# Splits ahead of what waits for the output projection, x loaded one group ahead, one store per head pair

## The chip, the cores and the metric

The kernel runs on one core of a Trainium2 chip. The metric is the time of one execution on the device in microseconds, the median of several runs. One more execution was recorded by the profiler; every row below is of that one. TensorE (PE; PEld is its weight load), VectorE (DVE), ScalarE (ACT) and GpSimd (POOL) compute, and SyncE (SP) issues all DMA transfers on one queue.

## The reference

Three blocks work on x, 64 sequences of 32 tokens with 512 features: cross attention to 257 context rows of 384 features per sequence, self attention with a relative position bias, and a quantised feed-forward network. The change touches the first one alone.

```python
def cross_attention(hidden_states, encoder_hidden_states, Wq, Wk, Wv, Wo, bo):   # 16 heads of 64
    q = hidden_states @ Wq
    k = encoder_hidden_states @ Wk
    v = encoder_hidden_states @ Wv
    scores = jnp.einsum('bhsd,bhkd->bhsk', q, k) * scale
    probs = jax.nn.softmax(scores, axis=-1)
    out = jnp.einsum('bhsk,bhkd->bhsd', probs, v)
    return out.transpose(0, 2, 1, 3).reshape(B, S, H * Dh) @ Wo + bo
...
x = x + cross_attention(_layernorm(x), ctx_768, ...)
x = x + self_attention(_layernorm(x), ...)
x = x + ffn(_layernorm(x), ...)
```

## The kernel before

Each engine has its own program, written out by hand, and semaphores order them. The eight PSUM banks (s0, s1, t0, t1, o0, o1, q0, q1) are handed round by a table: `full` waits until TensorE has filled a bank, `taken` until its reader has drained it. TensorE works in two-part arithmetic: every operand is kept as a high part, which ACT copies out, and a low part, the rest, which DVE subtracts out after it.

**Projection stage** (`*_project_all`). The 16 tiles of 128 tokens are taken in 4 groups. For each group x is loaded into one buffer `x_in` (`load_x_group`), normalised on DVE (`dve_group_stats` in the middle of the Q projections, `dve_group_norm` later; its step is counted in `s_xp`), transposed, multiplied by Wq (`Q`, eight units), and then by Wk of each head (`QK`, eight head pairs, units of 3 chunks x 2 heads), so that later the scores are taken directly against the context rows. The order of a group on TensorE is Q 0 to 3, QK 0 to 3, Q 4 to 7, transposes of the next group's x, QK 4 to 7. ACT copies the even head of a pair into the tile `staged`, DVE the odd one; `staged` has 4 slots, one per head pair, and `wait_slot` keeps a slot from being written before its last store has landed. SP stores each pair to `qk_by_tile` in DRAM, once it is complete, with one DMA per head (L1209), in rows of 1.5 KB.

**Main stage** (`*_cross_tile`). A tile is four batches, b = 0 to 3. For a batch TensorE makes scores against the context in four row groups (units S, bank order s0, s1, q0, s0), transposes of the probabilities of the batch before (PT, PL), their product with the context (PV 0 to 2), and three transposed chunks of the next context (CT 0 to 2). DVE takes row maxima (L1063), ACT the exponentials (L796), and a bank of scores is free when its exponential is done. In batch 1 the value projection W of the tile before is made, in batch 3 its output projection WO (L642), which stands between PV 1 and CT 2. DVE adds the residual to WO in `dve_x_out` (L1056). CT chunks are copied by ACT (L692) and DVE (L856) into `cT`; the chunk c = 2 is needed by the last three of the nine matmuls of the first scores of the next batch.

The projected q of tile t+1 lies in `raw` (one load of 3 MB, in batch 0 of tile t, after the last split has been done) and is split in batch 3 of tile t into `qk`: four high parts on ACT (`act_qk_high`, L730) and four low parts on DVE (`dve_qk_low`, L987), one per row group. GpSimd splits the context rows of each batch (`pool_split`, L1152 and L1155), after the last PV of the batch before; SP loads the context two batches ahead into one of two buffers `c_raw` after that (`load_ctx`, L1174).

In the lines of the tensors below, `c_raw_89` is the buffer of the even batches and `c_raw_98` of the odd ones.

Of the kernel before, what the change touches and what calls it, by code (L numbers as in the profile page):

```python
# [14 lines left out]
P = 128  # L15
# [133 lines left out]
def build_kernel(nc, x, ctx_768, Wq, Wk, Wv, Wo, bo, a_Wq, a_Wk, a_Wv, a_Wo, rel_emb, clip_x, clip_down,  # L149
# [22 lines left out]
    with ctx:  # L172
# [52 lines left out]
        assert sb.at <= STAGED  # L225
        staged = early("staged", [P, 4, 2, GROUP, HB], F32)
        x_in = early("x_in", [P, GROUP, D], F32)
# [469 lines left out]
        def wait_slot(eng, s, j):  # L697

            if 2 * s + j // 4:
                eng.wait_ge(s_staged[j % 4], 32 * (2 * s + j // 4))  # L700

# [7 lines left out]
        def act_group_qk(act, s, j):  # L709
            wait_slot(act, s, j)  # L710
            for c in range(KC):
                ps, free = full(act, project(("QK", s, j, c, 0)))
                nc.scalar.activation(staged[:, j % 4, 0, :, c * P:(c + 1) * P], tokens_of(ps), ACT.Copy).then_inc(free, 1)

# [12 lines left out]
        def act_qk_high(act, t, rg):  # L727

            act.wait_ge(s_qraw, 16 * t + 16)
            nc.scalar.activation(qk[:, 0, rg, :, :, :].rearrange("p c b (h q) -> p h (c b) q", h=4),  # L730
                                 raw[:, rg, :, :].rearrange("p h (a q) -> p h a q", q=SQ), ACT.Copy).then_inc(s_qhi, 1)

# [57 lines left out]
        def act_cross_tile(act, t, section):  # L790
# [16 lines left out]
            for b in range(4):  # L807
# [26 lines left out]
                act_last_scalars(act, b, 4 * t)  # L834
                if after:
                    ctxT(b, 2)
                if b == 3 and more:
                    act_qk_high(act, t + 1, 2)
                    act_qk_high(act, t + 1, 3)
                if section == "first" and b in (1, 2):  # L840
                    act_wo_high(act, b - 1)
# [120 lines left out]
        def dve_group_qk(dve, s, j):  # L962
            wait_slot(dve, s, j)
            for c in range(KC):
                ps, free = full(dve, project(("QK", s, j, c, 1)))
                nc.vector.tensor_copy(staged[:, j % 4, 1, :, c * P:(c + 1) * P], tokens_of(ps)).then_inc(free, 1)

# [13 lines left out]
        def dve_qk_low(dve, t, rg, section=None):  # L981

            if section:
                full(dve, U1(("S", 3, rg), t - 1, section))
            dve.wait_ge(s_qhi, 4 * t + (rg + 1))
            part = [qk[:, i, rg, :, :, :].rearrange("p c b (h q) -> p h (c b) q", h=4) for i in range(2)]
            nc.vector.tensor_tensor(part[1], raw[:, rg, :, :].rearrange("p h (a q) -> p h a q", q=SQ), part[0].bitcast(F32),  # L987
                                    ALU.subtract).then_inc(s_qlo, 1)
# [69 lines left out]
        def dve_cross_tile(dve, t, section):  # L1058
# [19 lines left out]
            for b in range(4):  # L1078
# [33 lines left out]
                if before:  # L1112
                    dve_attended(dve, t, b, 1, section)
                if b == 3 and begun:
                    dve_x_out(dve, t, section)
                if after:
                    ctxT(b, 2)
                if qk_next:
                    dve_qk_low(dve, t + 1, 2, section)
                if before:  # L1120
                    dve_attended(dve, t, b, 2, section)
                if qk_next:
                    dve_qk_low(dve, t + 1, 3, section)
                if section == "first" and b >= 2:
# [54 lines left out]
        def load_qk(sp, t, ahead):  # L1179
            later = qk_dram[ahead:]  # L1180
            one = later[t:t + 1] if isinstance(t, int) else later[bass.ds(t, 1)]
            sp.dma_start(raw[:].rearrange("p r h n -> p (r h n)"), one.rearrange("a p r h n -> p (a r h n)")).then_inc(s_qraw, 16)

        def sp_project_all(sp):
# [8 lines left out]
            load_ctx(sp, 0, 0)  # L1193
            load_ctx(sp, 0, 1)
            for s in range(GROUPS):
                if s < GROUPS - 1:
                    sp.wait_ge(s_xp, GROUP * (s + 1))
                    load_x_group(sp, s + 1)
                if s == 2:
                    sp.wait_ge(s_wqlo, 2)  # L1200
                    for i in range(4):
                        sp.wait_ge(s_staged[i], 64)
                    load_qk(sp, 0, 0)
                for j in range(8):
                    for c in range(KC):
                        for par in range(2):
                            taken(sp, project(("QK", s, j, c, par)))
                    for par in range(2):
                        sp.dma_start(qk_dram[GROUP * s:GROUP * (s + 1), :, 2 * (j // 4) + par, j % 4, :].rearrange("t p n -> p t n"),  # L1209
                                     staged[:, j % 4, par, :, :]).then_inc(s_staged[j % 4], 16)  # L1210
            for i in range(4):
                sp.wait_ge(s_staged[i], 64 * GROUPS)
            sp.dma_start(wv[:], Wv.rearrange("(k p) n -> p k n", p=P)).then_inc(s_wvo, 16)
# [4 lines left out]
        def sp_cross_tile(sp, t, section):  # L1218
            begun, more = section != "first", section != "last"
            for b in range(4):  # L1220
                if more or b < 2:
                    sp.wait_ge(s_nat, 4 * t + (b + 1))
                    load_ctx(sp, 4 * t, b + 2)
# [745 lines left out]
```

## Time and profile before

| | |
|---|---|
| median of 3 runs | 1853.93 us (1853.47 to 1854.21) |
| the profiled execution | 1855.51 us, span 1853.7 us |
| busy share: PE, DVE, ACT, POOL | 91%, 65%, 42%, 17% |
| mean granted TensorE clock | 0.956 |
| moved by DMA | 185.31 MB, 100 GB/s over the span |

The span is the time from the first to the last instruction on the core. A busy share counts instructions in flight over the whole span. The granted clock is given as a share of 2.4 GHz. The projection stage ends near 219 us, the main stage near 1172 us; tiles 1 to 14 are one loop, of which each pass is some 59 us.

### The profile page before, as it was taken

To read this page: it belongs to the slowest core of one execution; us is meant where nothing else is said; L and a number is where in the kernel's file an instruction comes from. 1 tells how busy PE (TensorE), PEld (TensorE's weight loads), DVE (VectorE), ACT (ScalarE), POOL (GpSimd) and SP (SyncE) were. 2 spreads that over 40 slices of the span, in tenths; PEclk is the share of its full clock that TensorE was granted. 3 is DMA by queue.
4 is the path that set the end of the run, shared out by engine and by line. 5 is a ranking of instruction groups with operands and counts; after the bars stand their busy time and mean duration, and the time that the engine had idled before them with its cause. 6 is when DMAs were issued, how large, how long until landed. Compare 5 with 4: busy or idle time off the path is not lost.

```text
span 1853.7 us, 38185 instructions
## 1 busy us (share of the span) xinstructions
PE 1693.4 (91%) x13767; PEld 1443.9 (78%) x13767; DVE 1207.7 (65%) x2675; ACT 780.8 (42%) x1699; POOL 315.7 (17%) x179
## 2 busy tenths in 40 slices
PE   6798879999999999999999999899999999996888
PEld 5677768888888888888888888789899998983333
DVE  6556656676666756666566666467777786646686
ACT  3343644445544544454544544232222222223556
POOL 0000022223222223232222223100000000000334
PEclk9998988999999999999999999999999999997899
DMA  4788852321222212221222212411111111003002
GB/s 168 271 288 309 310 194 95 105 105 37 102 105 105 95 37 103 105 105 39 100 105 105 75 55 75 176 53 40 45 40 45 40 45 35 17 23 113 31 16 91
DMA packets 81663, 185.31 MB, mean 100 GB/s; under 512 B 5008, under 2 KB 54224, under 8 KB 79568
## 3 DMA queue, kind: packets, MB, share of 16 engines
q1 hardware_dynamic: 81616, 184.68, 28.3%
q8 instruction: 30, 0.49, 0.1%
q14 instruction: 17, 0.14, 0.0%
HBM read 121.74 MB, written 62.91 MB: 100 GB/s over the span
## 4 chain that ended last, share of the span: by engine, by line
PE 53%; issue 31%; DVE 8%; ACT 3%; DMA 3%; SPq 1%; POOL 1%; DVEq 0%; ACTq 0%; POOLq 0%
PE psum_o L614 15%; PE psum_s L583 10%; PE psum_o L629 5%; PE psum_q L642 5%; PE psum_o L495 4%; PE psum_q L583 3%; PE psum_t L554 2%; DVE qk L987 2%; PE psum_t L594 2%; PE psum_o L1545 2%; DMA x_in<-in_x_dram 2%; PE psum_s L1545 2%; ACT qk L730 1%; PE psum_q L511 1%; PE psum_q L601 1%
## 5 line engine op out<-in xcount | busy, mean ns | idle before, releaser
L614 PE MATMUL psum_o<-pT,c_nat 128*128 128x512 f32 x1152 | 333.9, 430 | 10.3 <-issue 9.1
L583 PE MATMUL psum_s<-cT,qk 128*128 128x258 f32 x1728 | 256.7, 294 | 42.4 <-ACT probs L796 38.4
L583 PEld LDWEIGHTS psum_s<-cT,qk 128*128 128x128 f32 x1728 | 229.5, 194 | 55.7 <-ACT probs L796 39.0
L614 PEld LDWEIGHTS psum_o<-pT,c_nat 128*128 128x128 f32 x1152 | 219.7, 204 | 53.0 <-issue 12.1
L1152 POOL TENSOR_TENSOR c_nat<-c_raw,zero 128x768 fp32r<-128x768 f32 x64 | 94.9, 1483 | 899.2 <-PE psum_o L614 672.3
L1047 DVE SCALAR_TENSOR_TENSOR oT<-p_last,c_last,psum_o 128x512 f32<-128x512 f32 x192 | 142.8, 744 | 88.9 <-PE psum_o L614 88.7
L796 ACT ACTIVATE probs<-psum_s,nmax 128x257 f32<-128x257 f32 x192 | 91.8, 478 | 250.4 <-DVE nmax L1063 250.3
L987 DVE TENSOR_TENSOR qk<-raw,qk 128x1536 fp32r<-128x1536 f32 x64 | 141.0, 2205 | 15.9 <-ACT qk L730 15.6
L1155 POOL TENSOR_TENSOR c_nat<-c_raw,c_nat 128x768 fp32r<-128x768 f32 x64 | 140.8, 2200 | 5.0
L692 ACT ACTIVATE cT<-psum_t 128x256 fp32r<-128x256 f32 x192 | 68.3, 389 | 171.9 <-PE psum_t L554 171.5
L856 DVE TENSOR_TENSOR pT<-psum_t,pT 128x512 fp32r<-128x512 f32 x128 | 87.7, 686 | 71.0 <-ACT pT L692 71.0
L1267 PEld LDWEIGHTS psum_o<-xnT,w2q 128*128 128x128 f32 x1024 | 116.7, 192 | 2.4 <-issue 1.2
L1267 PE MATMUL psum_o<-xnT,w2q 128*128 128x128 f32 x1024 | 117.0, 275 | 1.0 <-issue 1.0
L1267 PE MATMUL psum_q<-xnT,w2k 128*128 128x128 f32 x1024 | 117.0, 275 | 0.0
L1267 PEld LDWEIGHTS psum_q<-xnT,w2k 128*128 128x128 f32 x1024 | 115.6, 192 | 0.0
L1063 DVE TENSOR_REDUCE nmax<-psum_s 128x1 f32<-128x257 f32 x192 | 80.4, 419 | 40.0 <-PE psum_s L583 40.0
L495 PE MATMUL psum_o<-xnT,wq 128*128 128x512 f32 x384 | 93.0, 402 | 4.9 <-DVE xnT L856 2.6
L730 ACT ACTIVATE qk<-raw 128x1536 fp32r<-128x1536 f32 x64 | 93.7, 1493 | 0.0
L495 PEld LDWEIGHTS psum_o<-xnT,wq 128*128 128x128 f32 x384 | 73.6, 194 | 23.4 <-issue 4.4
L629 PE MATMUL psum_o<-oT,wv 128*64 128x128 f32 x1536 | 90.7, 275 | 1.0 <-DVE oT L1047 1.0
L629 PEld LDWEIGHTS psum_o<-oT,wv 128*64 128x64 f32 x1536 | 83.2, 137 | 6.1 <-issue 4.0
L583 PE MATMUL psum_q<-cT,qk 128*128 128x258 f32 x576 | 82.7, 288 | 4.9 <-DVE qk L987 4.9
(225 smaller groups left out, 3098.3 us busy)
## 6 DMA issues: line engine op xcount, KB each, us to landing
qk_by_tile<-staged SPq DMA_DIRECT2D x64, 768.0 KB, 8.4
raw<-qk_by_tile SPq DMA_DIRECT2D x16, 3072.0 KB, 10.3
c_raw<-in_ctx_dram SPq DMA_DIRECT2D x64, 384.0 KB, 3.1
out_dram<-x_out SPq DMA_DIRECT2D x32, 256.0 KB, 2.0
x_in<-in_x_dram SPq DMA_DIRECT2D x4, 1024.0 KB, 10.4
x_res<-in_x_dram SPq DMA_DIRECT2D x16, 256.0 KB, 2.6
x_ln<-out_dram SPq DMA_DIRECT2D x16, 256.0 KB, 2.7
x_res<-out_dram SPq DMA_DIRECT2D x16, 256.0 KB, 2.9
```

The source lines that it names most:

```text
L495: m = pe.matmul(ps[:], wq[:, part, k, j * P:(j + 1) * P], xnT[:, moving, k, :, :], start=(k, part, moving) == (0, 0, 0), stop=(k, part) == ...
L583: m = pe.matmul(ps[:, 0:SKP], qk[:, part, rg, c, b, :], cT[b % 2][:, moving, c, :], start=(c, part, moving) == (0, 0, 0), stop=(c, part) = ...
L614: i = pe.matmul(ps[:], c_nat[(b - 1) % 2][:, part, k, m * P:(m + 1) * P], pT[:, moving, k, :], start=(k, part, moving) == (0, 0, 0), stop= ...
L629: i = pe.matmul(ps[64 * par:64 * par + 64, h4 * P:(h4 + 1) * P], wv[:, c, head * DH:(head + 1) * DH], oT[:, c, slot, :, :], start=c == 0, ...
L642: i = pe.matmul(ps[:], a[part][:, k, :], w[moving][:, k, :], start=(k, part, moving) == (0, 0, 0), stop=(k, part) == (KI - 1, 1))
L730: nc.scalar.activation(qk[:, 0, rg, :, :, :].rearrange("p c b (h q) -> p h (c b) q", h=4), raw[:, rg, :, :].rearrange("p h (a q) -> p h a ...
L796: nc.scalar.activation(probs[b % 2][:, rg, 0:SK], bank[bk][:, 0:SK], ACT.Exp, bias=nmax[:, rg:rg + 1], accum_out=den[:, rg:rg + 1]).then_i ...
L987: nc.vector.tensor_tensor(part[1], raw[:, rg, :, :].rearrange("p h (a q) -> p h a q", q=SQ), part[0].bitcast(F32), ALU.subtract).then_inc( ...
L1047: nc.vector.scalar_tensor_tensor(oT[:, m, :, (b - 1) % 4, :], p_last[:].rearrange("p (s q) -> p s q", q=SQ), c_last[:, (b - 1) % 2, m:m + ...
L1152: G.tensor_tensor(flat(c_nat[i][:, 0, :, :]), flat(c_raw[i][:]), zero[:].to_broadcast([P, 2 * DC]), ALU.add).then_inc(s_chi, 1)
L1155: G.tensor_tensor(c_nat[i][:, 1, :, :], c_raw[i][:], c_nat[i][:, 0, :, :].bitcast(F32), ALU.subtract).then_inc(s_nat, 1)
L1267: i = pe.matmul(ps[:, j * P:(j + 1) * P], w[:, k, (4 * n + j) * P:(4 * n + j + 1) * P], xnT2[:, k, :], start=k == 0, stop=k == KD - 1)
```

## The change

It has four parts.

The splits: in batch 3 of a tile, ACT makes the high parts of row groups 2 and 3 before it copies the third context chunk, and DVE makes their low parts directly behind the second attended chunk, ahead of `dve_x_out`, the third context chunk and the last attended chunk.

The loads of x: from group 2 on, x is loaded after the first four head pairs of the group two before have been stored, as soon as the group between has been normalised, and no longer at the start of the next group.

The stores: `staged`, `qk_by_tile` and `raw` have the two heads of a pair side by side, and one DMA stores both, in rows of 3 KB. The semaphore thresholds are halved.

The context of batch 2 of the first tile is loaded directly behind the last stores of the projection stage, ahead of the output and value weights.

```diff
-        staged = early("staged", [P, 4, 2, GROUP, HB], F32)
+        staged = early("staged", [P, 4, GROUP, 2, HB], F32)
...
             if 2 * s + j // 4:
-                eng.wait_ge(s_staged[j % 4], 32 * (2 * s + j // 4))
+                eng.wait_ge(s_staged[j % 4], 16 * (2 * s + j // 4))
...
                 act_last_scalars(act, b, 4 * t)
-                if after:
-                    ctxT(b, 2)
                 if b == 3 and more:
                     act_qk_high(act, t + 1, 2)
                     act_qk_high(act, t + 1, 3)
+                if after:
+                    ctxT(b, 2)
...
                     dve_attended(dve, t, b, 1, section)
+                if qk_next:
+                    dve_qk_low(dve, t + 1, 2, section)
+                    dve_qk_low(dve, t + 1, 3, section)
                 if b == 3 and begun:
                     dve_x_out(dve, t, section)
                 if after:
                     ctxT(b, 2)
-                if qk_next:
-                    dve_qk_low(dve, t + 1, 2, section)
                 if before:
                     dve_attended(dve, t, b, 2, section)
-                if qk_next:
-                    dve_qk_low(dve, t + 1, 3, section)
...
             load_ctx(sp, 0, 1)
+            sp.wait_ge(s_xp, GROUP)
+            load_x_group(sp, 1)
             for s in range(GROUPS):
-                if s < GROUPS - 1:
-                    sp.wait_ge(s_xp, GROUP * (s + 1))
-                    load_x_group(sp, s + 1)
...
-                    for par in range(2):
-                        sp.dma_start(qk_dram[GROUP * s:GROUP * (s + 1), :, 2 * (j // 4) + par, j % 4, :].rearrange("t p n -> p t n"),
-                                     staged[:, j % 4, par, :, :]).then_inc(s_staged[j % 4], 16)
+                    pair = qk_dram[GROUP * s:GROUP * (s + 1), :, j % 4, 2 * (j // 4):2 * (j // 4) + 2, :]
+                    sp.dma_start(pair.rearrange("t p r n -> p t (r n)"),
+                                 staged[:, j % 4, :, :, :].rearrange("p t r n -> p t (r n)")).then_inc(s_staged[j % 4], 16)
+                    if j == 3 and s < GROUPS - 2:
+                        sp.wait_ge(s_xp, GROUP * (s + 2))
+                        load_x_group(sp, s + 2)
+            sp.wait_ge(s_nat, 1)
+            load_ctx(sp, 0, 2)
             for i in range(4):
-                sp.wait_ge(s_staged[i], 64 * GROUPS)
+                sp.wait_ge(s_staged[i], 32 * GROUPS)
...
-                if more or b < 2:
+                if (more or b < 2) and (begun or b):
                     sp.wait_ge(s_nat, 4 * t + (b + 1))
                     load_ctx(sp, 4 * t, b + 2)
```

On DVE, at the end of the loop over the tiles (batch 3), the change moves these rows:

```order
-L1056 TENSOR_TENSOR x_out<-psum_q,x_res 128x512
-L855 REGISTER_ALU
-L856 TENSOR_TENSOR cT_87<-psum_t,cT_87 128x256
 L985 REGISTER_ALU
 L987 TENSOR_TENSOR qk<-raw,qk 128x4x12x32
-L1047 SCALAR_TENSOR_TENSOR oT<-p_last,c_last,psum_o 128x16x32
 L985 REGISTER_ALU
 L987 TENSOR_TENSOR qk<-raw,qk 128x4x12x32
...
+L1056 TENSOR_TENSOR x_out<-psum_q,x_res 128x512
+L855 REGISTER_ALU
+L856 TENSOR_TENSOR cT_87<-psum_t,cT_87 128x256
+L1047 SCALAR_TENSOR_TENSOR oT<-p_last,c_last,psum_o 128x16x32
```

Both low splits of q now stand ahead of the residual addition, the third context chunk and the last attended chunk.

On SP, from the load of x for group 1 to the load of q for tile 1, the rows were these before:

```order
L1177 DMA x_in<-in_x_dram 128x4x512
L1209 DMA qk_by_tile<-staged 128x4x384 x16
L1177 DMA x_in<-in_x_dram 128x4x512
L1209 DMA qk_by_tile<-staged 128x4x384 x16
L1177 DMA x_in<-in_x_dram 128x4x512
L1182 DMA raw<-qk_by_tile 128x6144
L1209 DMA qk_by_tile<-staged 128x4x384 x32
L1213 DMA wv<-in_L_xattn_Wv_dram 128x3x1024
L1214 DMA wo_raw<-in_L_xattn_Wo_dram 128x8x512
L1215 DMA bo_all<-in_L_xattn_bo_dram 128x512
L1216 DMA x_res<-in_x_dram 128x512
L1174 DMA c_raw_89<-in_ctx_dram 128x2x384
```

And in the changed kernel, whose lines have other numbers there, up to the same weights:

```order
L1176 DMA x_in<-in_x_dram 128x4x512
L1207 DMA qk_by_tile<-staged 128x4x768 x4
L1176 DMA x_in<-in_x_dram 128x4x512
L1207 DMA qk_by_tile<-staged 128x4x768 x8
L1176 DMA x_in<-in_x_dram 128x4x512
L1207 DMA qk_by_tile<-staged 128x4x768 x4
L1181 DMA raw<-qk_by_tile 128x6144
L1207 DMA qk_by_tile<-staged 128x4x768 x16
L1173 DMA c_raw_89<-in_ctx_dram 128x2x384
L1216 DMA wv<-in_L_xattn_Wv_dram 128x3x1024
L1217 DMA wo_raw<-in_L_xattn_Wo_dram 128x8x512
```

The loads of x stand half a group earlier among the stores, the stores are half as many and twice as wide, and the context load (`c_raw_89`) is ahead of the weights.

## Rows read from the trace of the kernel before

**Rows 1.** Waits in the loop's stretch: us in total, times, longest.
```profile
PE psum_s L583 <- ACT probs L796: 33.5, 14, 2.6
PE psum_q L583 <- DVE qk L987: 4.9, 14, 0.4
```

**Rows 2.** Windows of one tile, cut at its batches 0, 1, 2, 3.
```profile
core 0: us, PE busy (x) PEld busy (x) DVE busy (x) ACT busy (x) POOL busy (x), PEclk, DMA share, GB/s
341.54:357.00 15.46, 12.34 (x72) 10.59 (x71) 12.01 (x20) 7.59 (x20) 4.69 (x2) 0.89 0.71 250
357.00:373.62 16.62, 16.62 (x171) 15.04 (x169) 8.11 (x20) 7.08 (x20) 4.56 (x3) 1.00 0.10 35
373.62:384.09 10.47, 10.47 (x73) 9.57 (x72) 6.74 (x18) 5.66 (x18) 3.31 (x2) 1.00 0.12 38
384.09:399.97 15.88, 15.88 (x97) 14.06 (x96) 10.90 (x21) 8.87 (x21) 3.32 (x2) 1.00 0.09 25
```

**Rows 3.** Windows: 14 tile periods, a stretch behind one wait, self-attention stage.
```profile
341.02:1171.40 830.38, 783.64 (x5707) 696.47 (x5707) 526.82 (x1102) 405.88 (x1086) 222.42 (x126) 0.96 0.25 89
...
349.80:353.20 3.40, 3.02 (x11) 2.44 (x10) 2.48 (x8) 2.70 (x9) 0.00 (x0) 0.50 0.94 340
...
1195.00:1648.00 453.00, 449.45 (x5233) 409.92 (x5232) 321.92 (x920) 115.70 (x181) 0.46 (x1) 1.00 0.12 40
```

**Rows 4.** Timeline between tiles 1 and 2: start, duration, engine, line.
```profile
334.83 0.26 ACT L743 ACTIVATE c_last<-rem_sum 128x3 f32 x1
...
337.24 0.74 DVE L1047 SCALAR_TENSOR_TENSOR oT<-p_last,c_last,psum_o 128x512 f32<-128x512 f32 x1
...
340.13 0.69 DVE L1056 TENSOR_TENSOR x_out<-psum_q,x_res 128x512 f32<-128x512 f32 x1 [2.16 <-PE psum_q L642]
...
340.63 2.85 ACT L730 ACTIVATE qk<-raw 128x1536 fp32r<-128x1536 f32 x2
340.77 0.42 DVE L856 TENSOR_TENSOR cT<-psum_t,cT 128x256 fp32r<-128x256 f32 x1
...
341.54 1.24 PE L583 MATMUL psum_s<-cT,qk 128*128 128x258 f32 x9
...
341.88 1.47 POOL L1152 TENSOR_TENSOR c_nat<-c_raw,zero 128x768 fp32r<-128x768 f32 x1 [12.57 <-PE psum_o L614]
...
345.54 2.72 DVE L987 TENSOR_TENSOR qk<-raw,qk 128x1536 fp32r<-128x1536 f32 x1
...
348.19 0.41 DVE L1063 TENSOR_REDUCE nmax<-psum_s 128x1 f32<-128x257 f32 x1
...
349.25 1.90 PE L583 MATMUL psum_s<-cT,qk 128*128 128x258 f32 x9 [2.38 <-ACT probs L796]
```

**Rows 5.** The low splits of q on DVE: ns min/median/max, first and last start.
```profile
L987 DVE TENSOR_TENSOR qk<-raw,qk x64: 1736/1759/2820, 218.6 to 1116.4; 128x1536 fp32r<-128x1536 f32 x64
```

**Rows 6.** Windows from a group's first QK to its fifth: groups 1, 2, 0.
```profile
80.78:113.82 33.04, 23.90 (x139) 19.80 (x138) 18.30 (x44) 11.21 (x20) 0.00 (x0) 0.85 0.70 244
134.18:167.91 33.73, 24.40 (x138) 20.16 (x138) 18.39 (x44) 11.22 (x20) 0.00 (x0) 0.85 0.91 336
38.60:60.38 21.78, 21.59 (x137) 17.77 (x137) 16.99 (x42) 11.22 (x20) 0.00 (x0) 1.00 0.81 288
```

**Rows 7.** Timeline: the load of x for group 2, and its first reader.
```profile
75.49 2.32 SPq L1177 DMA_DIRECT2D x_in<-in_x_dram  x1
...
88.34 2.47 DVE L916 BATCH_NORM_STATS2 group_stats<-x_in 128x6 f32<-128x512 f32 x4 [8.85 <-DMA x_in<-in_x_dram]
```

**Rows 8.** Windows in which only stores, then only weight loads, are moved.
```profile
95.00:110.00 15.00, 15.00 (x84) 12.60 (x81) 10.25 (x31) 6.55 (x11) 0.00 (x0) 0.93 1.03 363
...
236.00:238.00 2.00, 2.00 (x19) 2.00 (x18) 1.17 (x5) 1.75 (x6) 0.00 (x0) 1.00 1.01 418
```

**Rows 9.** Timeline of TensorE: context transposes of batch 1 and batch 2, first tile.
```profile
248.13 1.11 PE L554 MATMUL psum_t<-ident,c_raw 128*128 128x128 f32 x4 [8.71 <-DMA c_raw<-in_ctx_dram]
...
261.43 0.60 PE L554 MATMUL psum_t<-ident,c_raw 128*128 128x128 f32 x4
```

**Rows 10.** DMA issue of batch 3's context, from about 239.1: KB, us to landing.
```profile
c_raw<-in_ctx_dram SPq DMA_DIRECT2D x1, 384.0 KB, 17.3
```

More of the change, by code:

```diff
@@ L712, in act_group_qk @@
                 ps, free = full(act, project(("QK", s, j, c, 0)))
-                nc.scalar.activation(staged[:, j % 4, 0, :, c * P:(c + 1) * P], tokens_of(ps), ACT.Copy).then_inc(free, 1)
+                nc.scalar.activation(staged[:, j % 4, :, 0, c * P:(c + 1) * P], tokens_of(ps), ACT.Copy).then_inc(free, 1)
         def act_wq_high(act, h):
@@ L730, in act_qk_high @@
             nc.scalar.activation(qk[:, 0, rg, :, :, :].rearrange("p c b (h q) -> p h (c b) q", h=4),
-                                 raw[:, rg, :, :].rearrange("p h (a q) -> p h a q", q=SQ), ACT.Copy).then_inc(s_qhi, 1)
+                                 raw[:, :, rg, :].rearrange("p h (a q) -> p h a q", q=SQ), ACT.Copy).then_inc(s_qhi, 1)
         def act_last_key(act, b, batch):
@@ L965, in dve_group_qk @@
                 ps, free = full(dve, project(("QK", s, j, c, 1)))
-                nc.vector.tensor_copy(staged[:, j % 4, 1, :, c * P:(c + 1) * P], tokens_of(ps)).then_inc(free, 1)
+                nc.vector.tensor_copy(staged[:, j % 4, :, 1, c * P:(c + 1) * P], tokens_of(ps)).then_inc(free, 1)
         def dve_wq_low(dve, h):
@@ L986, in dve_qk_low @@
             part = [qk[:, i, rg, :, :, :].rearrange("p c b (h q) -> p h (c b) q", h=4) for i in range(2)]
-            nc.vector.tensor_tensor(part[1], raw[:, rg, :, :].rearrange("p h (a q) -> p h a q", q=SQ), part[0].bitcast(F32),
+            nc.vector.tensor_tensor(part[1], raw[:, :, rg, :].rearrange("p h (a q) -> p h a q", q=SQ), part[0].bitcast(F32),
                                     ALU.subtract).then_inc(s_qlo, 1)
@@ L1181, in load_qk @@
             one = later[t:t + 1] if isinstance(t, int) else later[bass.ds(t, 1)]
-            sp.dma_start(raw[:].rearrange("p r h n -> p (r h n)"), one.rearrange("a p r h n -> p (a r h n)")).then_inc(s_qraw, 16)
+            sp.dma_start(raw[:].rearrange("p h r n -> p (h r n)"), one.rearrange("a p h r n -> p (a h r n)")).then_inc(s_qraw, 16)
         def sp_project_all(sp):
@@ L1201, in sp_project_all @@
                     for i in range(4):
-                        sp.wait_ge(s_staged[i], 64)
+                        sp.wait_ge(s_staged[i], 32)
                     load_qk(sp, 0, 0)
```

## The prediction

> **What bounds the kernel now.** I looked first at the waits of the main loop (tiles 1 to 15 of the cross attention), because nearly half of the span lies there. TensorE is busy for 783.64 of 830.38 us [rows 3], so it bounds the stage, and what can be saved is what it waits for and what it loses while its clock is halved. Its waits are few and regular: 14 times it waits for ACT's exponential (33.5 us in all, 2.4 us each), 14 times for a low split on DVE (4.9 us, 0.35 each) [rows 1]. Cutting one tile into its four batches shows where: batch 0 takes 15.46 us, batch 2, with the same work, 10.47 [rows 2]. Batches 1, 2 and 3 keep TensorE busy for every microsecond. So 5 us of each tile are lost at its start.
>
> The timeline of that start shows how [rows 4]. At the end of a tile DVE finishes with the second attended chunk at 337.98 (337.24 + 0.74) and then idles 2.16 us for the output projection (WO). ACT has been idle since 335.09. Only after WO do the last two splits of q for the next tile run: high parts on ACT from 340.63, low parts on DVE until 348.26 (345.54 + 2.72). The first row maximum of the new tile stands behind them, at 348.19. Its exponential frees bank s0, so the fourth block of scores, for which TensorE was ready at 346.87, starts at 349.25.
>
> The clock comes on top. Right behind this wait the granted clock is 0.50 (1.2 GHz, from 2.4), and it does not fall once in 453 us of the self-attention stage, where TensorE is busy 449 us [rows 3]. Over the loop the mean is 0.96: about 8% of 830 us, some 66 us, at half speed, which costs 33 us if TensorE has work throughout.
>
> **The moved splits.** I redo the boundary with the durations of the rows [rows 4]. ACT has nothing left to do at 335.09, so the two high splits (2.85 us) end at 337.95, well before the third context transpose reaches ACT. DVE starts the low splits at 337.98. One takes 1.76 us without a neighbour (median of 64), up to 2.82 beside GpSimd [rows 5]; GpSimd's own split starts only at 341.88 and two of DVE's end at 341.4, so 1.76 is the right one, with 0.5 us to spare. Then x_out (0.69) to 342.1, the low part of the third context chunk (0.42) to 342.5, attended chunk 2 (0.74, as the one at 337.24) to 343.2, row maximum to 343.6, exponential to 344.4. TensorE wants bank s0 at 346.5: that wait goes, and so does the one for the third split.
>
> What is late instead is the third context chunk: 342.5 where it was 341.2. TensorE starts the first scores at 341.54 and uses that chunk for the last three of nine matmuls, two thirds of 1.24 us later, at 342.35. I take a new wait of 0.2 us. Its bounds: nothing, and 2.1 us if both splits run beside GpSimd (1.0 each more). Behind the waiting matmul stand only TensorE's own transposes. x_out is stored 1.3 us later, and nobody in the loop waits for that store. The next tile's load of q, gated by the fourth split, only gets earlier.
>
> So batch 0 becomes batch 2 plus 0.2: a tile of 10.67 + 16.62 + 10.47 + 15.88 = 53.64 us. The loop's 830.38 us hold 14 tile periods with one boundary each, 59.31 on average. 14 x (59.31 - 53.64) = **79 us** saved. Of these about 46 are waits (2.4 + 0.35 + a cascaded half microsecond, less 0.2, per tile) and 33 the clock, which I take to stay up because nothing over 0.4 us remains.
>
> The Trainium skill, page "SBUF — State Buffer", section "SBUF: two separate sides", calls the port that DVE and GpSimd share an exclusive lock: the later of the two instructions blocks fully. The rows show the split stretched by 1.0 us at most, less than the 1.5 us of GpSimd's copy. By the page a split caught behind it would be late by the whole copy; by the rows, by 1.0 us.
>
> **x one group ahead.** In the projection stage, group 1 takes 33.04 us from its first QK to its fifth, and group 2 takes 33.73, where group 0 takes 21.78 for the same steps [rows 6]. The reason is one load: x for the next group is issued at 75.49, behind sixteen stores of the group before, and DVE, which takes its statistics in the middle of the Q projections, waits 8.85 us for it until 88.34 [rows 7]. All later copies out of PSUM stand behind, and TensorE with them. In the changed kernel the load goes out when that group's x is normalised, in front of the second four stores: for group 2 a transposition and some two Q projections before group 0's second QKs begin at 60.38, so about 55 us instead of 75. In front of it are at most the last of four stores, and it lands by about 64, some 15 us before DVE asks (88.34 - 8.85 = 79.5). SP now waits for the normalisation ahead of the second four stores, but these need QK results that begin later, at 60.38. Statistics of 2.5 us that now run on time push the copies by 0.3 us. Saved: 33.04 + 33.73 - 2 x 21.78 - 0.3 = **23 us**.
>
> **Rows of 3 KB.** The 32 stores move the same 50 MB. A half group is 6.3 MB, 17.3 us at the 363 GB/s of the stores; loads of longer rows reach 418 [rows 8]. So 3 KB rows save nothing to 2.3 us per half; I take 1.6 (400 GB/s). Nobody waits for a store in this trace, and a half group lasts 21 us, so the gain counts only at the end of the stage. The load of q for tile 0 (3 MB, 7.5 us) now runs into the stores of group 2, since TensorE no longer pauses there: the queue is then some 3 us behind. A slot is written again about 19 us after its store is issued (a half group less the way from the first copy to the store), and the last of four stores lands 3 + 15.7 - 6 + 2 = 15 us after its issue. That hides it; with that cover gone (1.5 KB rows and a queue 7 us behind), one wait of 1 to 3 us.
>
> The Trainium skill, page "DMA: Bandwidth & Descriptors", section "Specifications", puts the HBM limit of a core at 358 GB/s and line rate at 512 B rows; by it the longer rows would give 0. This trace's 418 GB/s is above it, but that is for loads, and no store here has longer rows. The sum would be lower by 1.6 us.
>
> **The context load.** In the first tile TensorE waits 8.71 us for the context of batch 2, until 248.13 [rows 9], because the load stood behind the weights. It now goes ahead of them, directly behind the last stores, and lands near 233, where 239.4 is needed. Late next is the context of batch 3: issued about 239.1, landing 17.3 us later at 256.4 [rows 10]. Everything in front of it starts 1.6 us earlier (stores) and is shorter by one context load (1.0 us), so it lands at 253.8. Its transposes stood at 261.43 [rows 9] and now run then: 7.6 us. On the way ACT waits for the output weights (bo lands last, about 244.7) with some 0.5 us for TensorE, inside this. At the end of this tile a low split of the weights (3.9 us) still keeps DVE, so its boundary gives only about 1 us, and the clock takes about as much back. **7.5 us**.
>
> **Sum.** 79 + 23 + 7.5 = 109.5 us from a span of 1853.7: 1744.2, in the profiled execution's time of 1855.5, 1746. The median of the runs is 1853.93, 1.6 us below that execution: **1744 us**.
>
> **Rivals.**
> *The clock still falls.* The waits go, but each tile still gets one stretch of 3.4 us or more at half speed, from the small waits at the boundary or the idle before it. For it: the loop has one such stretch in every tile. Against: they lie behind the 2.4 us wait. It gives back 1.7 to 2.4 us per tile, 24 to 33: 1768 to 1777. Chance 0.13.
> *GpSimd meets the splits.* If DVE is half a microsecond later than I reckon, its second split runs beside GpSimd, 1.0 us longer, and the first scores wait for the third chunk: 14 x 1.1 = 15 us, 1759. Chance 0.09. By the skill's lock it would be 1.5 us each, 21 us.
> *The change does not do it in the projections.* x still arrives late behind four stores, or a slot wait takes its place: up to 23 us back, 1767. Against: 15 us of slack. Chance 0.05.
> *Slower.* The third context chunk, attended 2 and the first row maximum all stand behind both splits now. Each microsecond by which the splits end after 341.4 is a microsecond of TensorE in the first scores, in each of 14 tiles. The loop's own gain is gone at 5.67 + 0.2 = 5.9 us of delay, all gains at 109.5 / 14 + 0.2 = 8 us; at 9 us the time is 1744 + 14 x 8.8 = 1867. It needs a late q or a held ACT. Against: q is loaded in batch 0 and split in batch 3, with 16.62 + 10.47 us of batches 1 and 2 between [rows 2]. Chance 0.02.
> *Forecast*: 0.71, by itself 1736 to 1754.
>
> **Numbers.** The range has 1732 below (no new wait, clock up in the first tile too, 12 us) and 1778 above (clock still falling). The measurement tells 0.2%, 3.7 us, from no change; every case but the slower one lies beyond it: faster 0.97, same 0.01, slower 0.02.
>
> **What would show it.** In the trace after: periods between stores of x_out near 53.6 us; batch 0 as long as batch 2; TensorE's wait for the exponential gone from the loop, in its place up to 0.2 us for the third chunk; mean clock of the loop 0.99 or 1.00; x in flight from about 55 us, no wait for it; the three group steps alike near 21.8 us; in the first tile a wait of some 3 us for the context of batch 3. I am wrong if the clock keeps falling once per tile, or if GpSimd's split starts before 341.4 on this scale.

## The result and the profile after

| | before | after |
|---|---|---|
| median of the runs | 1853.7 us (4 runs, 1853.13 to 1854.21) | 1738.15 us (4 runs, 1735.61 to 1741.85) |
| ratio, 95% interval | | 0.9378 (0.9359 to 0.9398) |
| profiled execution, its span | 1855.5, 1853.7 us | 1741.85, 1740.0 us |

The changed kernel is 115 us faster; the forecast was 110, and the time lies inside its range. The profiled execution is the slowest of its four runs, so the sums below, made in its time, come to 113.7 us. Line numbers after the change: GpSimd's copies of the context are L1151 and L1154, the stores of the projections L1207, the load of x L1176, that of q L1181, that of the context L1173.

The page of the changed kernel: first the span, then busy time by engine, then two rows of the DMA issues (KB each, median us to landing).

```profile
span 1740.0 us, 38153 instructions
...
PE 1650.0 (95%) x13767; PEld 1414.2 (81%) x13767; DVE 1173.3 (67%) x2675; ACT 779.3 (45%) x1699; POOL 297.3 (17%) x179
...
qk_by_tile<-staged SPq DMA_DIRECT2D x32, 1536.0 KB, 10.4
...
x_in<-in_x_dram SPq DMA_DIRECT2D x4, 1024.0 KB, 7.4
```

**The loop.** The windows of the loop's 14 periods, and of one tile cut at its four batches, in the changed kernel (columns as in [rows 2]).

```profile
310.48:1055.64 745.16, 745.16 (x5701) 671.92 (x5700) 491.19 (x1100) 402.23 (x1084) 202.63 (x126) 1.00 0.27 99
...
363.25:373.89 10.64, 10.64 (x73) 9.62 (x72) 7.35 (x20) 5.65 (x18) 3.31 (x2) 1.00 0.71 269
373.89:390.30 16.41, 16.41 (x170) 14.87 (x169) 8.12 (x20) 7.06 (x20) 4.55 (x3) 1.00 0.25 97
390.30:400.77 10.47, 10.47 (x74) 9.56 (x73) 6.74 (x18) 5.65 (x18) 3.31 (x2) 1.00 0.12 38
400.77:416.60 15.83, 15.83 (x97) 14.05 (x96) 13.37 (x22) 10.81 (x22) 3.32 (x2) 1.00 0.09 25
```

Against [rows 3] the loop is 85.2 us shorter: 46.7 of it is time in which TensorE was idle (830.38 less 783.64, now nothing), 38.5 is busy time (783.64 to 745.16). Most of that is the clock: cut into windows of 0.5 us, the loop before has 68.3 us at 0.50, in one stretch behind each of the 14 boundaries, and the changed loop has none. Half of it, 34.1 us, is the clock's part; the other 4.4 are not separated. Batch 0, 15.46 us in [rows 2], is now 10.64 and nearly as long as batch 2. A tile takes 53.35 us. The trace lists no wait of TensorE in this stretch; both of [rows 1] are gone.

The timeline of the boundary between tiles 1 and 2 in the changed kernel: start, duration, engine, line, and in brackets the idle time ahead and what ended it.

```profile
359.60 3.43 DVE L987 TENSOR_TENSOR qk<-raw,qk 128x1536 fp32r<-128x1536 f32 x2
...
362.93 0.69 DVE L1056 TENSOR_TENSOR x_out<-psum_q,x_res 128x512 f32<-128x512 f32 x1
...
363.25 1.39 PE L583 MATMUL psum_s<-cT,qk 128*128 128x258 f32 x9
...
363.53 0.42 DVE L856 TENSOR_TENSOR cT<-psum_t,cT 128x256 fp32r<-128x256 f32 x1
363.58 1.47 POOL L1151 TENSOR_TENSOR c_nat<-c_raw,zero 128x768 fp32r<-128x768 f32 x1 [12.58 <-PE psum_o L614]
...
367.85 1.32 PE L583 MATMUL psum_s<-cT,qk 128*128 128x258 f32 x9
```

The two splits now fill DVE's idle time ahead of the output projection and end at 363.03, 0.55 us before GpSimd starts (0.5 was reckoned). The first scores take 1.39 us instead of 1.24 [rows 4]: that is the new wait for the third context chunk, 0.15 us. The block at 367.85 is the one that waited 2.38 us in [rows 4]. Over the whole kernel, no split is stretched any more (the largest was 2820 ns in [rows 5]); min/median/max in ns:

```profile
L987 DVE TENSOR_TENSOR qk<-raw,qk x64: 1737/1754/1760, 195.1 to 1001.5; 128x1536 fp32r<-128x1536 f32 x64
```

**The projections.** Windows of groups 1, 2 and 0 in the changed kernel, cut as in [rows 6].

```profile
80.38:102.21 21.83, 21.63 (x137) 18.34 (x136) 16.86 (x42) 11.21 (x20) 0.00 (x0) 1.00 0.82 308
122.61:144.44 21.83, 21.63 (x137) 18.33 (x136) 16.86 (x42) 11.21 (x20) 0.00 (x0) 1.00 1.01 390
38.20:60.01 21.81, 21.61 (x137) 17.60 (x137) 17.01 (x42) 11.22 (x20) 0.00 (x0) 1.00 0.81 301
```

All three are alike. The timeline shows why: the load of x for group 2 is issued at 57.03 us, not at 75.49 [rows 7], and DVE's statistics start with no wait in brackets.

```profile
57.03 0.38 SPq L1176 DMA_DIRECT2D x_in<-in_x_dram  x1
...
79.00 2.46 DVE L916 BATCH_NORM_STATS2 group_stats<-x_in 128x6 f32<-128x512 f32 x4
```

**The first tile.** TensorE's waits there, changed kernel: the 8.71 us for batch 2's context [rows 9] are gone, and 4.33 us for batch 3's took their place. Later DVE's context chunks come late behind its splits of q. The 2.92 us were there before the change too. The 1.37 us are the price of the new order at this tile's end, where TensorE waited 4.2 us for the exponential before.

```profile
232.13 0.66 PE L554 MATMUL psum_t<-ident,c_raw 128*128 128x128 f32 x4 [4.33 <-DMA c_raw<-in_ctx_dram]
...
250.61 0.69 PE L554 MATMUL psum_t<-ident,c_raw 128*128 128x128 f32 x2 [2.92 <-DVE cT L856]
255.80 0.62 PE L583 MATMUL psum_s<-cT,qk 128*128 128x258 f32 x3 [1.37 <-DVE cT L856]
```

**The sum in the trace.** Up to the loop 30.5 us are saved (341.02 less 310.48), in the loop 85.2; behind the loop it is 2.1 us longer (1853.7 − 1171.40 = 682.3, 1740.0 − 1055.64 = 684.4). 30.5 + 85.2 − 2.1 = 113.6.

### The profile page after: what moved, and what is told of

Read it like the earlier page. It is cut to its first block, busy times and chain, and to the rows that moved or that the text cites. A ratio compares the mean times of both kernels' runs of the same rounds, so it can differ in the third digit from the quotient of the medians.

```text
span 1740.0 us, 38153 instructions
## 1 busy us (share of the span) xinstructions
PE 1650.0 (95%) x13767; PEld 1414.2 (81%) x13767; DVE 1173.3 (67%) x2675; ACT 779.3 (45%) x1699; POOL 297.3 (17%) x179
## 4 chain that ended last, share of the span: by engine, by line
PE 60%; issue 30%; DVE 5%; DMA 2%; ACT 2%; POOL 1%; SPq 0%; ACTq 0%; POOLq 0%; DVEq 0%
PE psum_o L614 15%; PE psum_s L583 11%; PE psum_o L629 5%; PE psum_q L642 5%; PE psum_o L495 5%; PE psum_q L583 4%; PE psum_t L594 3%; PE psum_t L554 2%; PE psum_o L1548 2%; PE psum_s L1548 2%; PE psum_q L601 2%; PE psum_t L511 1%; DMA c_raw<-in_ctx_dram 1%; PE psum_q L511 1%; PE psum_s L511 1%
## 5 line engine op out<-in xcount | busy, mean ns | idle before, releaser
L614 PE MATMUL psum_o<-pT,c_nat 128*128 128x512 f32 x1152 | 309.9, 406 | 3.8 <-issue 2.6
L583 PEld LDWEIGHTS psum_s<-cT,qk 128*128 128x128 f32 x1728 | 225.8, 190 | 17.5 <-issue 6.2
L614 PEld LDWEIGHTS psum_o<-pT,c_nat 128*128 128x128 f32 x1152 | 204.2, 190 | 39.2 <-DVE pT L856 3.4
L1151 POOL TENSOR_TENSOR c_nat<-c_raw,zero 128x768 fp32r<-128x768 f32 x64 | 95.4, 1490 | 801.9 <-PE psum_o L614 598.4
L1154 POOL TENSOR_TENSOR c_nat<-c_raw,c_nat 128x768 fp32r<-128x768 f32 x64 | 122.1, 1907 | 5.0
L987 DVE TENSOR_TENSOR qk<-raw,qk 128x1536 fp32r<-128x1536 f32 x64 | 110.6, 1751 | 1.7 <-ACT qk L730 1.5
L1349 PE MATMUL psum_t<-w2o_high,aT 128*128 128x512 f32 x256 | 84.2, 400 | 2.2 <-DVE aT L1451 2.2
```

What stands on the lines that cost most here:

```text
L583: m = pe.matmul(ps[:, 0:SKP], qk[:, part, rg, c, b, :], cT[b % 2][:, moving, c, :], start=(c, part, moving) == (0, 0, 0), stop=(c, part) = ...
L614: i = pe.matmul(ps[:], c_nat[(b - 1) % 2][:, part, k, m * P:(m + 1) * P], pT[:, moving, k, :], start=(k, part, moving) == (0, 0, 0), stop= ...
L987: nc.vector.tensor_tensor(part[1], raw[:, :, rg, :].rearrange("p h (a q) -> p h a q", q=SQ), part[0].bitcast(F32), ALU.subtract).then_inc( ...
L1151: G.tensor_tensor(flat(c_nat[i][:, 0, :, :]), flat(c_raw[i][:]), zero[:].to_broadcast([P, 2 * DC]), ALU.add).then_inc(s_chi, 1)
L1154: G.tensor_tensor(c_nat[i][:, 1, :, :], c_raw[i][:], c_nat[i][:, 0, :, :].bitcast(F32), ALU.subtract).then_inc(s_nat, 1)
```

## The experiments

**1. The moved splits alone, and each half.** `splits_only` is the kernel before with the moves on ACT and DVE:

```diff
 ACT:
-                if after:
-                    ctxT(b, 2)
                 if b == 3 and more:
                     act_qk_high(act, t + 1, 2)
                     act_qk_high(act, t + 1, 3)
+                if after:
+                    ctxT(b, 2)
 DVE:
+                if qk_next:
+                    dve_qk_low(dve, t + 1, 2, section)
+                    dve_qk_low(dve, t + 1, 3, section)
                 if b == 3 and begun:
                     dve_x_out(dve, t, section)
                 if after:
                     ctxT(b, 2)
-                if qk_next:
-                    dve_qk_low(dve, t + 1, 2, section)
                 if before:
                     dve_attended(dve, t, b, 2, section)
-                if qk_next:
-                    dve_qk_low(dve, t + 1, 3, section)
```

Expected: 

> The kernel before with the moved splits alone (ACT's and DVE's), all loads and stores as they were. If the splits do what the sum says, the loop gives all of its gain here: tile periods of 53.4 us instead of 59.3, no wait of TensorE for the exponential in the loop, mean clock of the loop 1.00, about 85 us less than before, 1768 us. If the loop's gain comes in part from the changed transfers (GpSimd's and SP's work meeting the boundary less), periods stay above 54.5 us and the time above 1784. If the waits go but the clock falls all the same, 46 us less: 1808.

Measured: 1763.84 us, ratio 0.9509 (0.9495 to 0.9523), about 91 us saved. Its loop, in the windows:

```profile
338.65:1083.88 745.23, 745.23 (x5701) 672.00 (x5700) 491.17 (x1100) 402.26 (x1084) 202.62 (x126) 1.00 0.27 99
```

745.23 against 745.16 us: the loop's whole gain is the splits'. The rest of the change adds nothing there.

Outside the loop the profiled `splits_only` is 2.4 us shorter ahead of it (341.02 less 338.65) and 2.6 behind it.

`act_half` has only ACT's part of that diff.

Expected: 

> The kernel before with ACT's half of the moved splits alone: the high parts 2 and 3 ahead of ACT's third context chunk, DVE's order as before. DVE's low splits still wait for the output projection, but no longer for ACT: the first starts at 341.2 instead of 342.1 on the scale of rows 4, so the wait of 2.4 us becomes 1.4. 0.95 us in 14 tiles are 13 us, 1840. If the shorter wait no longer makes the clock fall, 33 more: 1807.

Measured: 1799.57 us, ratio 0.9685 (0.9658 to 0.9713), 55 us saved by the medians and 58 by the ratio, more than either case expected (1840 and 1807). The windows, the waits (us in total, times, longest) and the timeline of `act_half` at a boundary:

```profile
338.91:1116.27 777.36, 756.55 (x5707) 677.12 (x5707) 504.58 (x1102) 401.81 (x1084) 234.06 (x126) 0.99 0.26 95
```

```profile
PE psum_o L614 <- issue: 13.0, 14, 0.9
PE psum_s L583 <- ACT probs L796: 7.8, 14, 0.6
```

```profile
394.24 1.75 DVE L987 TENSOR_TENSOR qk<-raw,qk 128x1536 fp32r<-128x1536 f32 x1
...
395.00 2.31 POOL L1152 TENSOR_TENSOR c_nat<-c_raw,zero 128x768 fp32r<-128x768 f32 x1 [12.58 <-PE psum_o L614]
...
396.56 2.37 DVE L987 TENSOR_TENSOR qk<-raw,qk 128x1536 fp32r<-128x1536 f32 x1
```

With the high parts ready early, DVE's third split no longer waits for ACT. It starts before GpSimd's copy instead of behind it, and then it is GpSimd that is stretched (2.31 instead of 1.47 us), while the split keeps its 1.75 (it was 2.8). The earlier start (1.0 us against TensorE's first scores), that microsecond and 0.35 us on the fourth split (2.37 for 2.72, [rows 4]) bring the exponential 2.5 us forward. TensorE itself comes 0.6 us earlier, so 0.55 us of the 2.38 us wait are left. What I had left out of both cases is that who starts first decides who is stretched.

The mean of 0.99 hides something. In windows of 0.5 us the clock still falls behind 3 of the 14 boundaries, 10.2 us in all, and at the other 11 it stays up. One boundary of each kind, with the same two waits ahead (0.55 us for the exponential and 0.94 ahead of the first PV):

```profile
402.50:405.80 3.30, 3.30 (x11) 2.62 (x10) 1.27 (x4) 2.40 (x9) 0.00 (x0) 0.50 1.11 457
458.00:461.30 3.30, 2.35 (x13) 1.93 (x13) 2.16 (x8) 2.94 (x11) 0.00 (x0) 1.00 0.98 343
```

`dve_half` has only DVE's part; it is the slower rival made true, since the low splits now wait for high splits that still follow the output projection.

Expected: 

> The kernel before with DVE's half of the moved splits alone: low parts 2 and 3 ahead of the residual, the third context chunk and the last attended chunk, while ACT still makes the high parts behind its third context chunk, which waits for the output projection. This is the slower rival made true: DVE's splits start at 342.1, run beside GpSimd to 347.6, the third context chunk is ready at 348.7, and TensorE waits in the first scores from 342.35, 6.4 us, with the half clock behind it. Batch 0 becomes 18.6 to 20.3 us instead of 15.5 to 17.6: 40 us more, 1894. If the order on DVE alone made the gain, about 1770.

Measured: 1894.07 us, ratio 1.0205 (1.0185 to 1.0224), as expected. The timeline of `dve_half` at a boundary:

```profile
401.85 6.09 DVE L987 TENSOR_TENSOR qk<-raw,qk 128x1536 fp32r<-128x1536 f32 x2 [4.16 <-ACT qk L730]
...
408.46 0.41 DVE L856 TENSOR_TENSOR cT<-psum_t,cT 128x256 fp32r<-128x256 f32 x1
...
408.93 1.01 PE L583 MATMUL psum_s<-cT,qk 128*128 128x258 f32 x3 [6.80 <-DVE cT L856]
```

This is the rival's mechanism in its place: two splits of 6.09 us, both beside GpSimd, hold the third context chunk, and TensorE waits 6.80 us in the middle of the first scores, 14 times 95.1 us in all. The loop has 103.4 us at half clock here, against 68.3 before. The half of DVE pays only together with that of ACT.

**2. The earlier loads of x alone.**

```diff
+            sp.wait_ge(s_xp, GROUP)
+            load_x_group(sp, 1)
             for s in range(GROUPS):
-                if s < GROUPS - 1:
-                    sp.wait_ge(s_xp, GROUP * (s + 1))
-                    load_x_group(sp, s + 1)
...
+                    if j == 3 and s < GROUPS - 2:
+                        sp.wait_ge(s_xp, GROUP * (s + 2))
+                        load_x_group(sp, s + 2)
```

Expected: 

> The kernel before with the earlier loads of x alone, stores in rows of 1.5 KB, two per head pair. By the sum: groups 1 and 2 take 21.8 us from their first QK to their fifth instead of 33.0 and 33.7, 23 us less, 1831 us. If the longer rows are needed for it (the queue of stores, with the 3 MB load of q behind them, then holds a staging slot), one or two waits of 1 to 3 us are left in group 2 and it gives 18 to 21 us.

Measured: 1833.06 us, ratio 0.9878 (0.9864 to 0.9893), about 22.6 us saved. The windows of groups 1 and 2:

```profile
80.64:102.44 21.80, 21.59 (x137) 18.32 (x137) 16.85 (x42) 11.22 (x20) 0.00 (x0) 1.00 0.90 314
122.79:144.61 21.82, 21.61 (x139) 18.05 (x138) 16.87 (x42) 11.21 (x20) 0.00 (x0) 1.00 1.03 378
```

So the whole effect is there with rows of 1.5 KB, and no wait for a slot appears: the cover of 15 us did not need the longer rows.

**3. The rows of 3 KB alone** (the layout of `staged`, one store per head pair, and the reading of q in that layout).

```diff
-                    for par in range(2):
-                        sp.dma_start(qk_dram[GROUP * s:GROUP * (s + 1), :, 2 * (j // 4) + par, j % 4, :].rearrange("t p n -> p t n"),
-                                     staged[:, j % 4, par, :, :]).then_inc(s_staged[j % 4], 16)
+                    pair = qk_dram[GROUP * s:GROUP * (s + 1), :, j % 4, 2 * (j // 4):2 * (j // 4) + 2, :]
+                    sp.dma_start(pair.rearrange("t p r n -> p t (r n)"),
+                                 staged[:, j % 4, :, :, :].rearrange("p t r n -> p t (r n)")).then_inc(s_staged[j % 4], 16)
```

Expected: 

> The kernel before with the 3 KB rows and one store per head pair alone; x, context and splits as they were. By the sum nobody waits for a store except at the end of the stage: nothing to 1.6 us less, 1852 to 1854. Rival: in this order the loads of x stand behind sixteen stores, so faster stores bring x forward too, 1.7 us for each of two groups, and 5 us in all are gained: 1849. By the rule that a core's HBM limit is 358 GB/s (Trainium skill, DMA: Bandwidth & Descriptors, Specifications) the stores do not get faster and it is 1854.

Measured: 1847.92 us, ratio 0.9966 (0.9953 to 0.9979), about 6.3 us saved; the rival was right. The windows of groups 1 and 2:

```profile
79.92:112.05 32.13, 24.06 (x138) 19.66 (x138) 18.33 (x44) 11.21 (x20) 0.00 (x0) 0.84 0.64 238
132.45:163.80 31.35, 23.55 (x137) 19.46 (x136) 18.32 (x44) 11.21 (x20) 0.00 (x0) 0.89 0.89 344
```

In the order of before, the load of x queues behind sixteen stores, so faster stores bring x earlier: 33.04 + 33.73 − 32.13 − 31.35 = 3.3 us of the group steps [rows 6]. The wait for batch 2's context falls from 8.71 to 7.37 us. With experiment 2 those 3.3 us can't be had twice: 91 + 22.6 + 6.3 + 2.6 (experiment 4) is 122.5, and the whole change gives 115. The rest of the difference is not separated.

**4. The earlier context load of the first tile alone.**

```diff
+            sp.wait_ge(s_nat, 1)
+            load_ctx(sp, 0, 2)
             for i in range(4):
                 sp.wait_ge(s_staged[i], 64 * GROUPS)
...
-                if more or b < 2:
+                if (more or b < 2) and (begun or b):
```

Expected: 

> The kernel before with the earlier load of the first tile's context of batch 2 alone. By the sum the wait of 8.7 us goes, and a wait for the context of batch 3 of some 4 us takes its place, which lands 1 us earlier than before: 6 us less, 1848. If the context of batch 3 is no limit, 10 us less, 1844. If the weights become the limit (ACT waiting for them ahead of its first weight split), less than 3 us.

Measured: 1851.9 us, ratio 0.9986 (0.9976 to 0.9996), about 2.6 us. The wait of 8.71 us is gone, and in the timeline this one took its place:

```profile
255.86 0.66 PE L554 MATMUL psum_t<-ident,c_raw 128*128 128x128 f32 x4 [4.18 <-DMA c_raw<-in_ctx_dram]
```

The loop starts 4.1 us earlier, half a microsecond of it because this execution started earlier. The new wait is the one expected, but the gain is less than half of the 6 us.

**5. TensorE kept busy through the wait.** The kernel before, with ten more matmuls of 128x512 in batch 0 of tiles 1 to 15, in front of the fourth block of scores. They write a bank that is overwritten afterwards; this adds work and leaves nothing out.

```diff
+                if b == 0 and begun:
+                    pe.wait_ge(s_wohi, 2)
+                    spare, _ = empty(pe, U1(("PV", 0, 0), t, section))
+                    for i in range(10):
+                        pe.matmul(spare[:], wo_high[:, 0, 0:P], wo_high[:, 1, :], start=True, stop=True)
                 pe_scores(pe, t, b, 3, section)
```

Expected: 

> The kernel before, unchanged but for ten matmuls of 512 columns put on TensorE ahead of the fourth block of scores of batch 0, where it waits 2.4 us in each tile; they write into the free bank of the next unit, which overwrites it. The wait stays on ACT and DVE, only TensorE is no longer idle in it. If the half clock comes from that idle stretch, the mean clock of the loop goes to 1.00, the tile period from 59.3 to about 57 us, and 33 us are gained: 1821. If the clock falls for another reason, 1854; if the extra work overruns the wait, more than 1854.

Measured: 1829.98 us, ratio 0.9863 (0.9844 to 0.9882), about 25 us faster with more work. The timeline of TensorE at one boundary, and the loop in the windows and the waits of `fill_wait`:

```profile
403.63 2.57 PE L665 MATMUL psum_o<-wo_high 128*128 128x512 f32 x10
406.27 1.34 PE L583 MATMUL psum_s<-cT,qk 128*128 128x258 f32 x9
```

```profile
340.45:1145.92 805.47, 787.71 (x5847) 698.94 (x5847) 524.88 (x1102) 403.45 (x1086) 222.40 (x126) 1.00 0.26 92
```

```profile
PE psum_o L614 <- issue: 11.8, 14, 0.9
PE psum_q L583 <- DVE qk L992: 4.9, 14, 0.4
```

With the idle stretch filled the clock stays at 1.00: it fell because of that stretch. Without the 36.0 us of the added matmuls (14 × 2.57) TensorE is busy 751.7 us, 32 us less than before; that is the 33 of the forecast. But idle and filled time together are 17.8 + 36.0 = 53.8 us where they were 46.7, so 7 us of it come back as waiting. The list of waits shows 3.5 of them ahead of PV: 11.8 us in 14 waits here, 8.3 us in 10 before, which [rows 1] do not list:

```profile
PE psum_o L614 <- issue: 8.3, 10, 0.9
```

I read it so: a faster TensorE arrives earlier at what other engines have ready at the same time as ever.

**6. The context of batch 3 ahead of the residual x and of q**, on the changed kernel.

```diff
+            sp.wait_ge(s_nat, 2)
+            load_ctx(sp, 0, 3)
             sp.dma_start(x_res[:], rows(x_rows, 0)).then_inc(s_xres, 16)
...
-                if (more or b < 2) and (begun or b):
+                if (more or b < 2) and (begun or b > 1):
```

Expected: 

> The changed kernel with one more load moved: the first tile's context of batch 3 goes ahead of the residual's x and of the 3 MB of q for tile 1. In the trace of the changed kernel TensorE waits 4.33 us for it. If the sum's step is right that this is what came late next, the wait goes, q is not missed, and 4 to 6 us are gained on the changed kernel, 1733. If the weights or ACT take its place, less than 2 us.

Measured: 1732.71 us (5 runs, 1730.3 to 1733.12), ratio 0.9335 to the kernel before (0.932 to 0.935). The waits of TensorE in the first tile:

```profile
PE psum_t L554 <- DVE cT L856: 2.9, 1, 2.9
PE psum_o L614 <- issue: 1.7, 2, 0.8
PE psum_s L583 <- DVE cT L856: 1.5, 1, 1.5
```

The 4.33 us are gone and the loop starts at 305.77 instead of 310.48 us. By the medians it is 5.4 us faster than the changed kernel, inside the 4 to 6 expected, and the fastest kernel of this study. What is left there waits mostly for DVE, behind its splits of q.

## Why the prediction was right, step by step

- **The moved splits: 79 us forecast, 85.2 in the loop.** The mechanism held at each place it named: splits in DVE's idle time, done 0.55 us before GpSimd, a new wait of 0.15 us (0.2 reckoned), batch 0 as long as batch 2, clock at 1.00. The waits come out at 46 (measured 46.7) only as the rest of the 79: the terms named, 2.4 + 0.35 + 0.5 − 0.2, give 43 in 14 tiles. The third of them is the wait ahead of PV (8.3 us in 10). The clock, 33, was worked out from a mean of 0.96, whose last digit alone is worth 4 us here; the 68.3 us at half clock make it 34.1, with 4.4 us more of busy time that nobody forecast. Seen by periods, the 5.8 us missing are these: the tile is 53.35 us and not 53.64 (13 × 0.29 = 3.8), and the last of the 14 periods is only 51.59 long (2.0 more). Most of the 0.29 is a cut in the wrong place: batch 1 was cut at 357.00, but its first scores start at 357.23:

```profile
357.23 1.24 PE L583 MATMUL psum_s<-cT,qk 128*128 128x258 f32 x9
```

- **"I take the clock to stay up because nothing over 0.4 us remains"**: right, and experiment 5 shows the cause. It also shows that the two terms are not worth their size apart: the clock alone gives 25 us. `act_half` shows how near the edge was: with waits of 0.55 and 0.94 us left, the clock still fell at 3 of 14 boundaries.
- **x one group ahead: 23 us forecast.** The last QK of the stage is at 192.94 instead of 216.40 us, 0.40 of it a different start: 23.06. Alone it gives 22.6.
- **Rows of 3 KB: "save nothing to 2.3 us per half", 1.6 taken.** In the sum it counted at the stage's end only. There the weights, which wait for the last store, are issued 15.8 us behind the start of the last QK (208.77 − 192.94) where it was 17.0 (233.38 − 216.40): 1.2 us of the 1.6. The rate was right too: 392 and 394 GB/s, 400 taken, 363 in [rows 8]. Wrong for the rows by themselves was "nobody waits for a store in this trace": the load of x did, in the queue.
- **The context load: 7.5 us forecast, 7.1 found** (30.54 up to the loop, less 23.46 up to the last QK). Its parts were off. The transposes of batch 3's context gained 5.8 us, not 7.6 (261.43 − 232.13 − 23.46): the load took 19.1 us to land, not 17.3 [rows 10], so the wait was 4.33 and not 3. The boundary gave more in turn, some 2.8 us instead of 1 (4.2 less 1.37). Alone the edit gives 2.6 us. The moved splits are not in that run, and what each part adds at the boundary was not separated.
- **Behind the loop, nothing was forecast and 2.1 us were lost**, all in the last 195 us, whose granted clock is 0.87, where it was 0.89. The runs do not show it as an effect of the change. The code there is the same in all ten kernels, and their profiled executions take 679.7 (`splits_only`) to 685.0 us (`x_only`) behind the loop, with that clock at 0.90 and 0.86; `ctx3_first`, which has the whole change, takes 680.0. What moves the clock there from one execution to the next is open.
- **Part of the small error is luck.** In the profiled execution's time 1746 was forecast and 1741.85 measured: the loop gave 6 us more and the stretch behind it 2 less. The median then lies 3.7 us below that execution, where 1.6 was taken.
- **The rivals.** *The clock still falls*: did not happen. *GpSimd meets the splits*: missed by 0.55 us. Its price, 1.0 us by the rows, was what the copy still had to run and no fixed amount; the last section has the count. *Slower*: `dve_half` shows it real, at 6.8 us per tile.

## What to carry to other kernels

Read the busiest stage tile by tile, and at the batch that is longer than its twin look for an engine that idles with ready work queued behind a wait; moving that work ahead of the wait pays, if it ends before what stood there is asked for and if all its producers move as well. A wait on TensorE can also cost the clock behind it, here 34 us for 47 us of waits. Part of that comes back as waiting, so measure the two together. Look for the half clock in short windows: a mean of 0.99 hid three stretches of it. A queue of stores delays the loads behind it even where nobody waits for a store.

## What the runs showed of the hardware

**The clock and an idle stretch.** With an idle stretch of 2.4 us in each tile the granted clock fell to 0.50 behind it [rows 3]. It did so at all 14 boundaries, 68.3 us in all. With the same stretch filled by matmuls it never fell in the loop (`fill_wait`). With the stretch cut to 0.55 us and 0.94 us of idling ahead of PV (`act_half`) it fell at 3 boundaries and not at the other 11. `fill_wait` has 0.85 us ahead of PV as well and no fall.

**DVE beside GpSimd.** A low split takes 1.75 us alone and up to 2.82 behind a running copy of GpSimd [rows 5]; over the whole of `dve_half` the longest takes 3.35:

```profile
L987 DVE TENSOR_TENSOR qk<-raw,qk x64: 1737/1759/3351, 216.9 to 1151.9; 128x1536 fp32r<-128x1536 f32 x64
```

Whichever of the two starts first keeps its time, and the later one loses what the earlier still had to run, less some 0.15 us. GpSimd's two passes take 1.47 and 1.84 us alone. At one boundary of the kernel before:

```profile
342.14 2.82 DVE L987 TENSOR_TENSOR qk<-raw,qk 128x1536 fp32r<-128x1536 f32 x1 [0.95 <-ACT qk L730]
343.43 3.22 POOL L1155 TENSOR_TENSOR c_nat<-c_raw,c_nat 128x768 fp32r<-128x768 f32 x1
```

The first pass has 1.21 us left (341.88 + 1.47 − 342.14) when the split starts, and the split loses 1.06. The split has 1.53 left when the second pass starts, and that pass loses 1.38. The next split (345.54, 2.72 us) meets 1.11 left and loses 0.96. In `act_half`, where the split is first, the copy meets 0.99 left and loses 0.84. Over the 14 boundaries of the kernel before and of `act_half` there are 84 such meetings, and in each the loss is 0.14 to 0.17 us less than what was left. By the Trainium skill, page "SBUF — State Buffer", section "SBUF: two separate sides", the later of the two is blocked fully. The trace agrees, in direction and, but for that 0.15 us, in size. The 1.0 us that the prediction read from [rows 5] is what a split lost that met 1.21 us of a copy, and no limit.

**Store rate by row length.** Three windows of the changed kernel in which stores keep the queue full, with rows of 3 KB:

```profile
65.00:75.00 10.00, 10.00 (x64) 8.22 (x62) 5.65 (x9) 4.97 (x9) 0.00 (x0) 1.00 1.03 394
88.00:98.00 10.00, 10.00 (x51) 8.14 (x48) 6.56 (x26) 3.16 (x6) 0.00 (x0) 1.00 1.03 394
170.00:180.00 10.00, 10.00 (x60) 8.43 (x57) 4.95 (x9) 4.78 (x8) 0.00 (x0) 1.00 1.03 392
```

Rows of 1.5 KB moved at 363 GB/s [rows 8]. The Trainium skill, page "DMA: Bandwidth & Descriptors", section "Specifications", gives 358 GB/s as the limit of a core and line rate from rows of 512 B. The traces show more than the first, 394 GB/s with one core at work; no run here has a second core beside it. On the second, the rate rose by 8% from 1.5 to 3 KB. The same edit also halved the number of DMAs and doubled the size of each, so no run shows which of the two raised it.
